# A decoder layer on one core: cross-attention's first steps with two pairs of projection banks, and the reload of the key norms in three steps

## Chip, cores and metric

The kernel runs on one core of one Trainium2 chip. The metric is device time in microseconds, the median of three runs; lower is better.

## What is computed

One pre-norm decoder layer on x (32 sequences of 64 tokens, 256 wide): self-attention with quantised projections, cross-attention over a context of 32 x 64 x 128, and a mixture of 8 experts, each added to x. The change touches cross-attention:

```python
q = (hidden_states @ Wq).reshape(B, Sq, H, D)          # H = 16 heads, D = 128
k = (encoder_hidden_states @ Wk).reshape(B, Skv, H, D)
v = (encoder_hidden_states @ Wv).reshape(B, Skv, H, D)
q = rmsnorm(q, gq)
k = rmsnorm(k, gk)
scores = jnp.einsum('bqhd,bkhd->bhqk', q, k) * scale
attn = jax.nn.softmax(scores, axis=-1)
out = jnp.einsum('bhqk,bkhd->bqhd', attn, v)
return out.reshape(B, Sq, H * D) @ Wo
```

The experts' part is `y = down(silu(gate(x)) * up(x))`, with weights of 8 experts that the kernel splits into two float16 halves (a high part and what is left of it) before it uses them.

## The kernel before

Three stages run one after another with a barrier between them: self-attention (0 to 229 us of the trace), cross-attention (230 to 625 us), experts (625 to 963 us).

Cross-attention handles 64 heads, numbered h: 4 groups of 512 tokens by 16 heads. Heads go in pairs. A loop over steps N from -9 to 32 is written out by hand for each engine; in step N the projections of pair m = N + 9 are made, the scores of pair n = N + 1, and the outputs of pair N. So the first eight steps, N = -9 to -2, only project pairs 0 to 7, which are the 16 heads of the first group; the step of N = -1 brings the first scores, and from N = 1 on every step has all parts.

For one head TensorE (PE) makes, in `query`, six matmuls of 512 columns into `bank_q`, and in `key` three into `bank_k` (L1051, L1059). ScalarE (ACT) squares the query bank and copies its high half (L857, L858), and squares the key bank (L864). VectorE (DVE) makes the query's low half (`query_low`, L960) and both halves of the key (`key_halves`, L964 and L966). In `squares` PE sums the squares into `bank_n` (L1071, 8 small matmuls in float32). There is one `bank_q` and one `bank_k`, so the query product of head h waits until DVE has read that of head h - 1 (`lq_done`), and the key product likewise (`lk_done`). The squares of the queries go to two buffers in turn, those of the keys to one, `sqk`. Accumulators `acc[0]` and `acc[1]` are two more banks, first written in the step of N = 1, by `project_out`.

**Pieces.** Beside this the experts' weights are prepared: 67 pieces of 128 x 512 float32, two for each step from N = -8 to N = 24 and one in N = 25. SyncE's queue (SP) loads a piece (`piece_load`, L765), ACT makes its high half (`piece_high`, L903), the low half comes from DVE for even pieces (L1003) and from GpSimd (POOL) for odd ones (two instructions, L826 and L828), and SP saves both halves to DRAM (`piece_save`, L769) and then at once loads piece i + 2 into the same buffer. There are two raw buffers, one for even and one for odd pieces. ACT does both pieces of a step at the step's start, ahead of everything else of that step.

**Key norms.** After 8 heads (a batch b, in the steps of m = 4, 8, ..., 32) ACT turns the summed squares into norms (L872, L876, and L883 for the queries). The keys' norms go through DRAM so that they come back spread over partitions: `key_norms(b)` on SP issues four saves (L777), waits until they have landed, and issues eight loads (L788, 128 KB each) into the tile `rec_k`, which lies in `ao`; two for each pair u. GpSimd multiplies them with the queries' norms (`both_norms`, L810), two steps ahead of the pair's scores in the first loop and three in the last steps.

SP's order in a step is: save even piece, load, save odd piece, load, and then `key_norms` where a batch is due. Whatever stands there holds up the saves and loads of the step behind it.

Of the kernel before, what the change touches and what calls it, by code (L numbers as in the profile page):

```python
# [24 lines left out]
LN_EPS = 1e-5  # L25


IDENT, ONES, SAMEB, POS, PICK0, PICK1, BEFORE, CONSTS = 0, 128, 256, 384, 448, 576, 704, 832

# [640 lines left out]
def cross_attention(nc, sem, over, dram, x_sb, cst, ao, hT, wq, wk, wvo, cT, ck):  # L670
# [6 lines left out]
    with ctx:  # L677
# [5 lines left out]
        kc = sb("x_kc", [P, P], F32)  # L683
        gains = sb("x_gains", [P, 5], F32)
        sqq = [sb(f"sqq{i}", [P, GN], F32) for i in range(2)]
        sqk = sb("sqk", [P, GN], F32)
        sc = [sb(f"x_sc{i}", [P, 2 * GT, S], F32) for i in range(2)]
        pf = sb("x_pf", [P, 2 * GT, S], F32)
        mx = [sb(f"x_mx{i}", [P, 2 * GT], F32) for i in range(2)]
# [60 lines left out]
        def bank_of(n):  # L750
            return bank_s if n <= TAIL else bank_n

        nc.clear_and_free_semaphores(over)
        with nc.Block() as block:

            @block.sync
            def _(sp):
                sp.dma_start(gains[:, 0:1], dram["gq2"].rearrange("(p a) -> p a", a=1)).then_inc(g_in, 16)
                sp.dma_start(gains[:, 1:2], dram["gk2"].rearrange("(p a) -> p a", a=1)).then_inc(g_in, 16)
                def piece_load(i):  # L760
                    if i == early:

                        sp.wait_ge(q_done, H2)
                        sp.wait_ge(k_done, H2)
                    sp.dma_start(raw(i), dram["wx"][:, i * PIECE:(i + 1) * PIECE]).then_inc(raw_in[i % 2], 16)  # L765

                def piece_save(i):
                    sp.wait_ge(low_odd if i % 2 else low_even, i // 2 + 1)
                    sp.dma_start(dram["w_hl"][:, :, i * PIECE:(i + 1) * PIECE].rearrange("l p n -> p l n"), halves(i)).then_inc(pair_out[i % 2], 16)  # L769
                    if piece(i + 2):  # L770
                        piece_load(i + 2)

                def key_norms(b):
                    g, first = b * HB // H2, b * HB % H2
                    sp.wait_ge(kc_done, b + 1)
                    for t in range(GT):
                        sp.dma_start(dram["key_norms"][g % 2].rearrange("b h t s -> t h b s")[t, first:first + HB],  # L777
                                     kc[32 * t + first:32 * t + first + HB, :].rearrange("h (b s) -> h b s", b=2)).then_inc(kc_saved, 16)
                    sp.wait_ge(kc_saved, (b + 1) * GT * 16)
                    if g:  # L780
                        sp.wait_ge(s_read, (b * HB - H2 + HB) // 2)
                    if b == 1:

                        for r in range(2):
                            sp.wait_ge(pair_out[r], early // 2 * 16)
# [66 lines left out]
            def _(act):  # L852
                def query(h):
                    act.wait_ge(q_done, h + 1)
                    if h >= 2:
                        act.wait_ge(ss_done, h - 1)
                    nc.scalar.activation(sqq[h % 2][:, :], bank_q, ACT.Square, scale=1.0 / (H_UP * W_UP)).then_inc(sq_done, 1)  # L857
                    nc.scalar.copy(q_hl[:, 0, slot(h), :], bank_q).then_inc(hq_done, 1)  # L858
# [90 lines left out]
            def _(dve):  # L949
# [7 lines left out]

                def query_low(h):
                    dve.wait_ge(hq_done, h + 1)
                    nc.vector.tensor_tensor(q_hl[:, 1, slot(h), :], bank_q, q_hl[:, 0, slot(h), :], ALU.subtract).then_inc(lq_done, 1)  # L960

                def key_halves(h):
                    dve.wait_ge(sq_done, h * 2 + 2)
                    nc.vector.tensor_scalar(k_hl[:, 0, slot(h), :], bank_k, gains[:, 2:3], None, ALU.mult).then_inc(hk_done, 1)  # L964
                    dve.wait_ge(hk_done, h + 1)
                    nc.vector.scalar_tensor_tensor(out=k_hl[:, 1, slot(h), :], in0=bank_k, scalar=gains[:, 2:3], in1=k_hl[:, 0, slot(h), :], op0=ALU.mult, op1=ALU.subtract).then_inc(lk_done, 1)  # L966

                def out_low(h):
                    dve.wait_ge(oh_done, h + 1)
# [73 lines left out]
            @block.tensor  # L1043
            def _(pe):
                def query(h):
                    if h:
                        pe.wait_ge(lq_done, h)
                    f, g = h % H2 * D2, h // H2
                    terms = [(k, a, b) for k in range(NCH) for a, b in TERMS]
                    for j, (k, a, b) in enumerate(terms):  # L1050
                        last = nc.tensor.matmul(bank_q, wq[:, a, k, f:f + D2], hT[:, g, b * NCH + k, :], start=(j == 0), stop=(j == len(terms) - 1))  # L1051
                    last.then_inc(q_done, 1)

                def key(h):
                    if h:
                        pe.wait_ge(lk_done, h)
                    f, g = h % H2 * D2, h // H2
                    for j, (a, b) in enumerate(TERMS):
                        last = nc.tensor.matmul(bank_k[:, :], wk[:, a, f:f + D2], cT[:, g, b, :], start=(j == 0), stop=(j == 2))  # L1059
                    last.then_inc(k_done, 1)  # L1060

                def squares(h):
# [3 lines left out]

                        pe.wait_ge(rq_done, h // HB)
                    pick = cst[:, PICKH + 31 - e:PICKH + 63 - e]
                    for i, sq in enumerate((sqq[h % 2], sqk)):
# [82 lines left out]
                for N in steps:  # L1152
# [490 lines left out]
def constants():  # L1643

    import numpy as np
    p, m, s = np.arange(P)[:, None], np.arange(P)[None, :], np.arange(S)[None, :]
    parts = [p == m, p >= 0 * m, p // S == m // S, p % S == s, p == m % S, p == S + m % S, p < m]
# [80 lines left out]
```

## Time and profile before

| what | value |
|---|---|
| median of 3 runs | 962.99 us (962.37 to 966.84) |
| profiled execution, its own time | 964.96 us |
| its span, first to last instruction | 963.2 us |
| mean granted TensorE clock | 0.921 of full |
| busy: PE / DVE / ACT / POOL | 787.8 / 632.4 / 535.6 / 386.0 us |
| the first eight steps of cross-attention | 233.2 to 301.4 us |

The profile lists for each engine when it was busy and, for each pause ahead of an instruction, what ended it. A pause matters where the engine in question, or one that waits for it, is the late one.

### The profile page before, as it was taken

The numbers are of one execution on the slowest core, as the hardware profiler recorded it, in microseconds if no ns is written. First come the engines' busy times: TensorE is split into PE (matmuls) and PEld (weight loads), VectorE is DVE, ScalarE is ACT, GpSimd is POOL, SyncE is SP. The second block draws the span as 40 slices with busy tenths as digits, with TensorE's granted clock in tenths as the row PEclk, the third lists the DMA queues.
The fourth block names the chain that finished last, engine by engine and source line by source line (L and its number), as shares of the span: only waits on it lengthen the run. The fifth ranks groups of instructions, "written<-read, shape, count | busy, mean of one in ns | idle before, by whom it ended". The sixth has DMA issues, their size and how long they took to land. (4 is left out here: it accounts for less than half of the span.)

```text
span 963.2 us, 29306 instructions
## 1 busy us (share of the span) xinstructions
PE 787.8 (82%) x11741; PEld 578.0 (60%) x11741; DVE 632.4 (66%) x1110; ACT 535.6 (56%) x1002; POOL 386.0 (40%) x445
## 2 busy tenths in 40 slices
PE   0599988864767999999999988862599999999992
PEld 0488878751323566566656656662477777777771
DVE  6788999553656899989999988667433333333330
ACT  1687878742545777676767664431155445445541
POOL 0231222320334555555555556300336555555542
PEclk9998999955998999999999989955799999999997
DMA  9110000000453444434243432092492222222223
GB/s 330 44 47 24 25 24 25 26 1 22 132 165 100 134 132 133 125 98 134 94 146 116 134 104 76 2 361 89 148 359 46 39 40 46 44 37 43 45 35 103
DMA packets 59402, 92.18 MB, mean 96 GB/s; under 512 B 6769, under 2 KB 39665, under 8 KB 59089
## 3 DMA queue, kind: packets, MB, share of 16 engines
q1 hardware_dynamic: 48048, 76.49, 23.9%
q0 software_dynamic: 7488, 10.23, 6.6%
q10 hardware_dynamic: 3744, 3.67, 1.1%
q8 instruction: 98, 1.61, 0.7%
q14 instruction: 24, 0.19, 0.1%
HBM read 63.36 MB, written 29.10 MB: 96 GB/s over the span
## 5 line engine op out<-in xcount | busy, mean ns | idle before, releaser
L1528 DVE SCALAR_TENSOR_TENSOR hid<-psu,hid 128x688 f32<-128x688 f32 x39 | 34.1, 875 | 146.3 <-ACT hid L1390 146.3
L1051 PE MATMUL xbank_qk<-arena 128*128 128x512 f16 x384 | 97.7, 392 | 20.8 <-DVE q_hl L960 15.8
L1146 PE MATMUL xbank_a<-arena,x_o 128*128 128x256 f16 x768 | 95.7, 275 | 2.8 <-DVE x_sb L999 1.7
L1390 ACT ACTIVATE hid<-psg 128x688 f32<-128x688 f32 x39 | 29.0, 744 | 117.3 <-PE psu L1597 117.3
L1612 PE MATMUL fbank<-arena,hidT 128*128 (+1 forms) x663 | 82.8, 273 | 0.8 <-ACT f_y L1410 0.8
L1146 PEld LDWEIGHTS xbank_a<-arena,x_o 128*128 128x128 f16 x768 | 72.6, 98 | 18.0 <-DVE x_o L970 7.8
L857 ACT ACTIVATE sqq<-xbank_qk 128x512 f32<-128x512 f32 x64 | 38.2, 597 | 78.0 <-PE xbank_qk L1051 78.0
L1597 PE MATMUL psg<-wgu,f_xT 128*128 x468 | 75.0, 310 | 4.0 <-ACT f_xT L1397 2.2
L1597 PE MATMUL psu<-wgu,f_xT 128*128 x468 | 74.6, 309 | 0.0
L1612 PEld LDWEIGHTS fbank<-arena,hidT 128*128 128x128 f16 (+1 forms) x663 | 62.9, 97 | 15.4 <-issue 9.2
L1051 PEld LDWEIGHTS xbank_qk<-arena 128*128 128x128 f16 x384 | 33.0, 99 | 63.2 <-DVE q_hl L960 23.9
L1364 POOL DMA_INDIRECT token_out<-f_y,f_to x39 | 62.6, 1604 | 17.3 <-issue 16.8
L1059 PE MATMUL xbank_qk<-cT,wk 128*128 128x512 f16 x192 | 53.5, 388 | 12.9 <-DVE k_hl L966 12.9
L817 POOL TENSOR_TENSOR x_pf<-x_sc,x_rden 128x512 f32<-128x512 f32 x32 | 33.4, 1043 | 75.5 <-DVE x_rden L993 75.5
L960 DVE TENSOR_TENSOR q_hl<-xbank_qk,q_hl 128x512 f16<-128x512 f32 x64 | 43.7, 682 | 24.0 <-ACT q_hl L858 24.0
L1597 PEld LDWEIGHTS psu<-wgu,f_xT 128*128 128x128 f16 x468 | 45.8, 98 | 22.5
L1597 PEld LDWEIGHTS psg<-wgu,f_xT 128*128 128x128 f16 x468 | 42.6, 98 | 27.7 <-issue 4.8
L826 POOL TENSOR_SCALAR arena<-arena 128x512 f32<-128x512 f32 x25 | 37.7, 1507 | 53.4 <-ACT x_pair L903 53.4
L964 DVE TENSOR_SCALAR k_hl<-xbank_qk,x_gains 128x512 f16<-128x512 f32 x64 | 47.8, 747 | 11.1 <-ACT sqk L864 11.1
L538 PE MATMUL bank_pt<-cst,sp 64*64 64x64 f32 x1024 | 42.2, 240 | 13.1 <-ACT pT L299 11.7
L1347 POOL COPY f_at<-f_from_all 128x1 uint32 (+1 forms) x39 | 27.1, 695 | 63.3 <-DVE f_from_all L1508 52.6
L966 DVE SCALAR_TENSOR_TENSOR k_hl<-xbank_qk,x_gains,k_hl 128x512 f16<-128x512 f32 x64 | 48.1, 751 | 2.3
(257 smaller groups left out, 1955.1 us busy)
## 6 DMA issues: line engine op xcount, KB each, us to landing
arena<-in_wx SPq DMA_DIRECT2D x51, 256.0 KB, 3.7
wgu<-w_hl SPq DMA_DIRECT2D x8, 1376.0 KB, 9.0
ao<-key_norms SPq DMA_DIRECT2D x64, 128.0 KB, 3.2
w_hl<-cT SPq DMA_DIRECT2D x26, 256.0 KB, 2.1
w_hl<-x_pair SPq DMA_DIRECT2D x25, 256.0 KB, 3.4
ao<-in_wx SPq DMA_DIRECT2D x16, 256.0 KB, 3.0
w_hl<-ao SPq DMA_DIRECT2D x16, 256.0 KB, 2.1
arena<-w_hl SPq DMA_DIRECT2D x8, 384.0 KB, 8.8
```

What stands on the lines that cost most here:

```text
L538: last = nc.tensor.matmul(pt[rows, n * S:(n + 1) * S], sp[i % 2][rows, 8 * part + n, :], cst[rows, IDENT + S * b:IDENT + S * b + S], start ...
L826: nc.gpsimd.tensor_scalar(raw(i), raw(i), W_UP, None, ALU.mult).then_inc(up_done, 1)
L857: nc.scalar.activation(sqq[h % 2][:, :], bank_q, ACT.Square, scale=1.0 / (H_UP * W_UP)).then_inc(sq_done, 1)
L960: nc.vector.tensor_tensor(q_hl[:, 1, slot(h), :], bank_q, q_hl[:, 0, slot(h), :], ALU.subtract).then_inc(lq_done, 1)
L964: nc.vector.tensor_scalar(k_hl[:, 0, slot(h), :], bank_k, gains[:, 2:3], None, ALU.mult).then_inc(hk_done, 1)
L966: nc.vector.scalar_tensor_tensor(out=k_hl[:, 1, slot(h), :], in0=bank_k, scalar=gains[:, 2:3], in1=k_hl[:, 0, slot(h), :], op0=ALU.mult, o ...
L1051: last = nc.tensor.matmul(bank_q, wq[:, a, k, f:f + D2], hT[:, g, b * NCH + k, :], start=(j == 0), stop=(j == len(terms) - 1))
L1059: last = nc.tensor.matmul(bank_k[:, :], wk[:, a, f:f + D2], cT[:, g, b, :], start=(j == 0), stop=(j == 2))
L1146: last = nc.tensor.matmul(acc[t // 2][:, (t % 2) * C:(t % 2 + 1) * C], o_hl[h % 2][:, a, at:at + P], wvo[:, b, e, :], start=(e == 0 and j ...
L1364: nc.gpsimd.indirect_dma_start(out=dram["token_out"], out_offset=bass.IndirectOffsetOnAxis(ap=to[:, 0:1], axis=0), in_=y[r ^ 1][:, :], in_ ...
L1597: last = nc.tensor.matmul(bank[:, c * 512:c * 512 + FH], xT[r][:, b * NCH + k, :], wgu[:, bass.ds(e, 1), at:at + FH].rearrange("p a n -> p ...
L1612: last = nc.tensor.matmul(ps[1][:, 0:C], hidT[r][0:rows, a, f, :], wd[0:rows, bass.ds(e, 1), at:at + C].rearrange("p a n -> p (a n)"), sta ...
```

## The change

- In the first eight steps the odd head of a pair is projected into `acc[0]` (query) and `acc[1]` (key) instead of `bank_q` and `bank_k`. A product of these steps waits for the reader of the head before the last (`banks_free`).
- PE's order in these steps: the key product of the odd head stands ahead of the squares of the even head.
- The keys' squares get a second buffer; ACT's key square waits for the sums of the head before the last, in all steps.
- `key_norms` is cut in three: saves in the batch's step, the loads of pairs u, u + 1 at the end of the next step, those of the other two pairs at the end of the one after.
- Four constant tables that nothing reads leave the constants' tile: 448 columns of 1113.

```diff
-IDENT, ONES, SAMEB, POS, PICK0, PICK1, BEFORE, CONSTS = 0, 128, 256, 384, 448, 576, 704, 832
+IDENT, ONES, BEFORE, CONSTS = 0, 128, 256, 384
...
-        sqk = sb("sqk", [P, GN], F32)
+        sqk = [sb(f"sqk{i}", [P, GN], F32) for i in range(2)]
...
+        def query_bank(h):
+            return acc[0][:, :] if h < H2 and h % 2 else bank_q
+
+        def key_bank(h):
+            return acc[1][:, :] if h < H2 and h % 2 else bank_k
+
+        def banks_free(h):
+            return h if h > H2 else h - 1
...
-                def key_norms(b):
+                def key_norms_out(b):
                     g, first = b * HB // H2, b * HB % H2
                     sp.wait_ge(kc_done, b + 1)
                     for t in range(GT):
...
+
+                def key_norms_in(b, part):
+                    g, first = b * HB // H2, b * HB % H2
                     sp.wait_ge(kc_saved, (b + 1) * GT * 16)
...
-                    for u in range(first // 2, (first + HB) // 2):
+                    for u in range(first // 2 + 2 * part, first // 2 + 2 * part + 2):
...
                     if batch(N) is not None:
-                        key_norms(batch(N))
+                        key_norms_out(batch(N))
+                    for part in range(2):
+                        if batch(N - 1 - part) is not None:
+                            key_norms_in(batch(N - 1 - part), part)
...
                 def key(h):
                     act.wait_ge(k_done, h + 1)
-                    if h:
-                        act.wait_ge(ss_done, h)
-                    nc.scalar.activation(sqk[:, :], bank_k, ACT.Square, scale=1.0 / (CTX_UP * W_UP)).then_inc(sq_done, 1)
+                    if h >= 2:
+                        act.wait_ge(ss_done, h - 1)
+                    nc.scalar.activation(sqk[h % 2][:, :], key_bank(h), ACT.Square, scale=1.0 / (CTX_UP * W_UP)).then_inc(sq_done, 1)
...
                 def query(h):
-                    if h:
-                        pe.wait_ge(lq_done, h)
+                    if banks_free(h) > 0:
+                        pe.wait_ge(lq_done, banks_free(h))
...
                 def key(h):
-                    if h:
-                        pe.wait_ge(lk_done, h)
+                    if banks_free(h) > 0:
+                        pe.wait_ge(lk_done, banks_free(h))
...
                         query(2 * m + 1)
+                        if m < NU:
+                            key(2 * m + 1)
                         squares(2 * m)
-                        key(2 * m + 1)
+                        if m >= NU:
+                            key(2 * m + 1)
```

The same order, as the engines get it. TensorE, one of the first eight steps, before (`xbank_qk` holds `bank_q` and `bank_k`, `xbank_n` is `bank_n`, `arena` holds the queries' weights and inputs):

```order
L1051 MATMUL xbank_qk<-arena 128x512 x6
L1059 MATMUL xbank_qk<-cT,wk 128x512 x3
L1051 MATMUL xbank_qk<-arena 128x512 x6
L1071 MATMUL xbank_n<-sqq,cst 32x128 x4
L1071 MATMUL xbank_n<-sqk,cst 32x128 x4
L1059 MATMUL xbank_qk<-cT,wk 128x512 x3
L1071 MATMUL xbank_n<-sqq,cst 32x128 x4
L1071 MATMUL xbank_n<-sqk,cst 32x128 x4
```

and in the changed kernel (`xbank_a` is the pair of accumulators; its line numbers are 16 higher here):

```order
L1067 MATMUL xbank_qk<-arena 128x512 x6
L1075 MATMUL xbank_qk<-cT,wk 128x512 x3
L1067 MATMUL xbank_a<-arena 128x512 x6
L1075 MATMUL xbank_a<-cT,wk 128x512 x3
L1087 MATMUL xbank_n<-sqq,cst 32x128 x4
L1087 MATMUL xbank_n<-sqk,cst 32x128 x4
L1087 MATMUL xbank_n<-sqq,cst 32x128 x4
L1087 MATMUL xbank_n<-sqk,cst 32x128 x4
```

The four products now stand together, and both sums of squares behind them.

SyncE's queue from the load that ends the step of m = 4 on, before (L765 loads a piece, L769 saves one, L777 and L788 save and load norms):

```order
L777 DMA key_norms<-x_kc 8x2x64 x4
L788 DMA ao<-key_norms 64x512 x8
L769 DMA w_hl<-ao 128x2x512
L765 DMA ao<-in_wx 128x512
L769 DMA w_hl<-ao 128x2x512
L765 DMA ao<-in_wx 128x512
L769 DMA w_hl<-ao 128x2x512
```

and in the changed kernel (L775 loads a piece, L779 saves one, L787 and L801 save and load norms):

```order
L787 DMA key_norms<-x_kc 8x2x64 x4
L779 DMA w_hl<-ao 128x2x512
L775 DMA ao<-in_wx 128x512
L779 DMA w_hl<-ao 128x2x512
L775 DMA ao<-in_wx 128x512
L801 DMA ao<-key_norms 64x512 x4
L779 DMA w_hl<-ao 128x2x512
L775 DMA ao<-in_wx 128x512
L779 DMA w_hl<-ao 128x2x512
L775 DMA ao<-in_wx 128x512
L801 DMA ao<-key_norms 64x512 x4
```

The eight loads that stood as one block ahead of the next piece's save now follow that step's and the next step's piece loads, four and four.

## Rows read from the trace of the kernel before

**Rows 1.** The page, its first part: TensorE, share of the span, instructions.
```profile
PE 787.8 (82%) x11741; PEld 578.0 (60%) x11741; DVE 632.4 (66%) x1110; ACT 535.6 (56%) x1002; POOL 386.0 (40%) x445
```

**Rows 2.** Busy time by stretch: PE, PEld, DVE, ACT, POOL (count), clock, DMA share, GB/s.
```profile
242.00:249.40 7.40, 5.47 (x54) 2.26 (x50) 4.99 (x8) 4.18 (x8) 2.64 (x2) 1.00 0.47 141
286.00:292.80 6.80, 6.11 (x42) 2.16 (x43) 2.99 (x5) 2.71 (x5) 1.01 (x1) 0.50 0.31 96
```

**Rows 3.** Waits in 233 to 301.4 us: total us, times, longest us.
```profile
PE xbank_qk L1051 <- DVE q_hl L960: 12.8, 8, 4.5
PE xbank_n L1071 <- ACT sqk L864: 5.5, 8, 0.7
```

**Rows 4.** Timeline, odd piece's loop; start us, us, engine, line [idle before <-releaser].
```profile
254.51 0.47 SPq L765 DMA_DIRECT2D ao<-in_wx  x1
...
257.57 0.63 ACT L903 ACTIVATE ao<-ao 128x512 f16<-128x512 f32 x1 [0.63 <-DMA ao<-in_wx]
...
258.28 1.65 POOL L826 TENSOR_SCALAR ao<-ao 128x512 f32<-128x512 f32 x1 [4.22 <-ACT ao L903]
...
260.01 1.15 POOL L828 TENSOR_TENSOR ao<-ao 128x512 f16<-128x512 f32 x1
...
261.61 0.47 SPq L765 DMA_DIRECT2D ao<-in_wx  x1
...
264.56 0.63 ACT L903 ACTIVATE ao<-ao 128x512 f16<-128x512 f32 x1 [0.20 <-DMA ao<-in_wx]
```

**Rows 5.** Timeline, first two pieces on ACT.
```profile
241.28 1.14 ACT L903 ACTIVATE ao<-ao 128x512 f16<-128x512 f32 x2
```

**Rows 6.** Timeline, the reload of the norms and what follows.
```profile
268.45 0.47 SPq L765 DMA_DIRECT2D ao<-in_wx  x1
268.96 1.41 SPq L777 DMA_DIRECT2D key_norms<-x_kc  x4
...
272.32 4.99 SPq L788 DMA_DIRECT2D ao<-key_norms  x8
...
279.02 0.56 SPq L765 DMA_DIRECT2D ao<-in_wx  x1
...
283.57 0.63 ACT L903 ACTIVATE ao<-ao 128x512 f16<-128x512 f32 x1 [0.65 <-DMA ao<-in_wx]
...
285.94 2.74 PE L1051 MATMUL xbank_qk<-arena 128*128 128x512 f16 x6 [4.52 <-DVE q_hl L960]
```

**Rows 7.** Line L765: landing of the load issued at 245.68, then of all 67.
```profile
DMA to landing us min/median/max: 4.9/4.9/4.9
...
DMA to landing us min/median/max: 2.8/3.6/5.3
```

**Rows 8.** Timeline, the step of N = -1 and the start of the next.
```profile
300.66 1.14 ACT L903 ACTIVATE ao<-ao 128x512 f16<-128x512 f32 x2
...
303.78 0.60 ACT L857 ACTIVATE sqq<-xbank_qk 128x512 f32<-128x512 f32 x1 [1.27 <-PE xbank_qk L1051]
...
310.98 0.95 PE L1099 MATMUL xbank_s<-k_hl,q_hl 128*64 128x64 f16 x48
```

**Rows 9.** Timeline, two pauses of TensorE and what follows each.
```profile
306.42 1.47 PE L1051 MATMUL xbank_qk<-arena 128*128 128x512 f16 x6 [1.92 <-DVE q_hl L960]
...
572.88 1.04 PE L1113 MATMUL xbank_s<-x_identh,x_p 128*128 128x128 f16 x8 [3.60 <-POOL x_p L822]
```

**Rows 10.** The page's GB/s in 40 slices; timeline, last stats of x.
```profile
GB/s 330 44 47 24 25 24 25 26 1 22 132 165 100 134 132 133 125 98 134 94 146 116 134 104 76 2 361 89 148 359 46 39 40 46 44 37 43 45 35 103
...
16.36 1.40 DVE L382 BATCH_NORM_STATS2 stats<-x_sb 128x6 f32<-128x256 f32 x4 [0.47 <-DMA x_sb<-in_x]
```

**Rows 11.** Timeline, a later piece that ACT waited for.
```profile
409.36 0.63 ACT L903 ACTIVATE cT<-arena 128x512 f16<-128x512 f32 x1 [1.09 <-DMA arena<-in_wx]
```

**Rows 12.** Timeline, the last save, and the product of norms 29.
```profile
590.77 0.37 SPq L769 DMA_DIRECT2D w_hl<-cT  x1
...
595.34 1.51 POOL L810 TENSOR_TENSOR ao<-ao,rec_q 128x512 f32<-128x512 f32 x1
```

More of the change, by code:

```diff
@@ L856, in query @@
                         act.wait_ge(ss_done, h - 1)
-                    nc.scalar.activation(sqq[h % 2][:, :], bank_q, ACT.Square, scale=1.0 / (H_UP * W_UP)).then_inc(sq_done, 1)
-                    nc.scalar.copy(q_hl[:, 0, slot(h), :], bank_q).then_inc(hq_done, 1)
+                    nc.scalar.activation(sqq[h % 2][:, :], query_bank(h), ACT.Square, scale=1.0 / (H_UP * W_UP)).then_inc(sq_done, 1)
+                    nc.scalar.copy(q_hl[:, 0, slot(h), :], query_bank(h)).then_inc(hq_done, 1)
                 def key(h):
                     act.wait_ge(k_done, h + 1)
-                    if h:
-                        act.wait_ge(ss_done, h)
-                    nc.scalar.activation(sqk[:, :], bank_k, ACT.Square, scale=1.0 / (CTX_UP * W_UP)).then_inc(sq_done, 1)
+                    if h >= 2:
+                        act.wait_ge(ss_done, h - 1)
+                    nc.scalar.activation(sqk[h % 2][:, :], key_bank(h), ACT.Square, scale=1.0 / (CTX_UP * W_UP)).then_inc(sq_done, 1)
                 def out_high(h):
@@ L959, in query_low @@
                     dve.wait_ge(hq_done, h + 1)
-                    nc.vector.tensor_tensor(q_hl[:, 1, slot(h), :], bank_q, q_hl[:, 0, slot(h), :], ALU.subtract).then_inc(lq_done, 1)
+                    nc.vector.tensor_tensor(q_hl[:, 1, slot(h), :], query_bank(h), q_hl[:, 0, slot(h), :], ALU.subtract).then_inc(lq_done, 1)
                 def key_halves(h):
                     dve.wait_ge(sq_done, h * 2 + 2)
-                    nc.vector.tensor_scalar(k_hl[:, 0, slot(h), :], bank_k, gains[:, 2:3], None, ALU.mult).then_inc(hk_done, 1)
+                    nc.vector.tensor_scalar(k_hl[:, 0, slot(h), :], key_bank(h), gains[:, 2:3], None, ALU.mult).then_inc(hk_done, 1)
                     dve.wait_ge(hk_done, h + 1)
-                    nc.vector.scalar_tensor_tensor(out=k_hl[:, 1, slot(h), :], in0=bank_k, scalar=gains[:, 2:3], in1=k_hl[:, 0, slot(h), :], op0=ALU.mult, op1=ALU.subtract).then_inc(lk_done, 1)
+                    nc.vector.scalar_tensor_tensor(out=k_hl[:, 1, slot(h), :], in0=key_bank(h), scalar=gains[:, 2:3], in1=k_hl[:, 0, slot(h), :], op0=ALU.mult, op1=ALU.subtract).then_inc(lk_done, 1)
                 def out_low(h):
@@ L1050, in query @@
                     for j, (k, a, b) in enumerate(terms):
-                        last = nc.tensor.matmul(bank_q, wq[:, a, k, f:f + D2], hT[:, g, b * NCH + k, :], start=(j == 0), stop=(j == len(terms) - 1))
+                        last = nc.tensor.matmul(query_bank(h), wq[:, a, k, f:f + D2], hT[:, g, b * NCH + k, :], start=(j == 0), stop=(j == len(terms) - 1))
                     last.then_inc(q_done, 1)
                 def key(h):
-                    if h:
-                        pe.wait_ge(lk_done, h)
+                    if banks_free(h) > 0:
+                        pe.wait_ge(lk_done, banks_free(h))
                     f, g = h % H2 * D2, h // H2
                     for j, (a, b) in enumerate(TERMS):
-                        last = nc.tensor.matmul(bank_k[:, :], wk[:, a, f:f + D2], cT[:, g, b, :], start=(j == 0), stop=(j == 2))
+                        last = nc.tensor.matmul(key_bank(h), wk[:, a, f:f + D2], cT[:, g, b, :], start=(j == 0), stop=(j == 2))
                     last.then_inc(k_done, 1)
@@ L1068, in squares @@
                     pick = cst[:, PICKH + 31 - e:PICKH + 63 - e]
-                    for i, sq in enumerate((sqq[h % 2], sqk)):
+                    for i, sq in enumerate((sqq[h % 2], sqk[h % 2])):
                         for t in range(GT):
@@ L1645, in constants @@
     import numpy as np
-    p, m, s = np.arange(P)[:, None], np.arange(P)[None, :], np.arange(S)[None, :]
-    parts = [p == m, p >= 0 * m, p // S == m // S, p % S == s, p == m % S, p == S + m % S, p < m]
+    p, m = np.arange(P)[:, None], np.arange(P)[None, :]
+    parts = [p == m, p >= 0 * m, p < m]
     c = np.concatenate([np.asarray(x, np.float32) for x in parts], axis=1)
```

## The prediction

> **What bounds the kernel now.** First the page: TensorE is busy 82% of the span [rows 1], so the question is where it is not. Two stretches of cross-attention's first steps answer it [rows 2]. From 242.0 to 249.4 us, one step of the eight (it runs from an even head's query product to the next even head's), TensorE works 5.47 of 7.4 us, VectorE 4.99, ScalarE 4.18, GpSimd 2.64: nobody is full, so a chain of waits sets the step. From 286.0 to 292.8 us the granted clock is 0.50, which is 1.2 GHz, half of the 2.4 GHz of the other. The view of waits names the chain [rows 3]: in these eight steps TensorE stood still 8 times, 12.8 us in all, ahead of a query product until VectorE had read the bank, and 8 times, 5.5 us, ahead of the squares until ScalarE had squared the key. The first kind is what a second pair of banks takes away.
>
> Then I look for a second loop nearly as long, because one that was hidden becomes the bound. It is the odd piece's [rows 4]: load issued at 254.51, ScalarE starts on it at 257.57, having stood 0.63 us for that transfer, GpSimd at 258.28 and again at 260.01, next load issued at 261.61 (1.6 us after the second GpSimd instruction's start, the save between them), ScalarE at 264.56, again after a wait, of 0.20 us. That is 7.0 us from one odd piece to the next, in a chain in which TensorE has no part; the step takes 7.4. ScalarE does its pieces at a step's start, ahead of all projections of the step, so it can't go faster than this loop.
>
> The third thing is the reload of the norms [rows 6]. SP issues the four saves at 268.96, then waits for them, and the eight loads start at 272.32 and take 4.99 us to issue. The odd piece's load comes at 279.02, 10.6 us after the one before it, of 268.45, its piece reaches ScalarE at 283.57, and TensorE, after a pause of 4.52 us, starts at 285.94 and needs 2.74 us for six matmuls that take 1.47 us at full clock [rows 9]. This one reload costs the late pieces and then the half clock.
>
> **The change, part by part.** Everything below is in the profiled execution, whose 964.96 us stand 1.97 above the median; the sum is a difference, and I take it off the median, 962.99.
>
> *Start of the chain.* ScalarE's first two pieces start at 241.28, the odd one some 0.5 us later, 241.8 [rows 5]. They stand behind the key square of head 1. In this step TensorE's second query product loses its wait (1.6 us in the mean [rows 3], of which I take 0.9 here, since the key product ahead of it still runs at the low clock), and the key product no longer stands behind the squares. Those take 0.5 us a head: 5.47 us less 18 long matmuls at 1.47 us for six leaves 1.06 for two heads [rows 2, 9]. So the first odd piece starts 1.4 us sooner, at **240.4**.
>
> *Seven turns of the odd loop.* Before, they took from 241.8 to 301.2 [rows 5, 8] (300.66, and 0.5 for the even one), 59.4 us. After, each is 7.0 us at least [rows 4]. One of the landings was slow, 4.9 us instead of the 3.0 usual here, and nothing of the change touches it [rows 7]: +1.8. For the load that runs beside the four saves of norms I add 0.4; for the two that start just ahead of or behind the blocks of four norm loads, 1.1 and 0.7 (their landing beside the eight was 4.5 us, 283.57 less 279.02 [rows 6], so 1.5 each is the upper end, nothing the lower). Together 49.0 + 1.8 + 2.2 = **53.0 us**, and 293.4 for the last odd piece instead of 301.2. Is SP free in time? Four loads of norms take half of 4.99, so 2.5 us; a step of 7 us has only four short issues beside, and by the loop's own times there are some 3 us between an odd load and the next even save. So the block of four just fits, and the reload's 3.6 us of lateness and the half clock behind it go. The wait for the saves to land is over a step later.
>
> *The step of N = -1.* Before, ScalarE's pieces here were not late; the query's square began at 303.78 and the next scores at 310.98, 7.2 us later [rows 8]. After, this step hangs on the odd piece: it is followed by 1.4 us of ScalarE (the piece, the logarithm, the exponential) and the same 7.2 us. So the next scores start at 240.4 + 53.0 + 8.6 = **302.0 instead of 310.98: 9.0 us less.**
>
> *A pause that is new.* Head 17 is past the double banks and waits for the reader of head 16, which now waits for the late odd piece. TensorE is there a step ahead, so I work out a pause of 3.8 to 4.0 us. After 3.60 us it came back at half clock (eight transposes in 1.04 us [rows 9]), after 1.92 us at full clock. Six matmuls at half clock cost 1.27 more, part of it beside VectorE's work: **+0.6**, with 0 and 2 as ends.
>
> *Steady steps, N = 0 to 23.* TensorE bounds them and their products keep one pair of banks. What goes is a late piece behind some reloads: ScalarE waited 1.09 us at 409.36 [rows 11], and a like amount once more. I take **-0.7**, between 0 and -2.3. The second `sqk` buffer I cost at nothing: the wait it relaxes, for sums that TensorE makes before the key product it follows, was always over.
>
> *Tail.* The last batch's second block of loads now stands behind the last save, at 590.77 [rows 12]. Pair 30 needs it; pair 29 was at 595.34 and a step is over 5 us, so it is due at about 600.7. Two issues and a landing, by 595.6: **0**, with 5 us to spare.
>
> *Constants.* 448 columns of 4 bytes on 128 partitions are 229 KB; at the 330 GB/s of the first slice 0.7 us, and VectorE waited 0.47 us for the last of x [rows 10]: **-0.5**, between 0 and -0.7.
>
> Sum: -9.0 + 0.6 - 0.7 - 0.5 = **-9.6 us, so 953.4** (about 955.4 if the profiled execution again stands 2 above).
>
> The Trainium skill (DMA: Bandwidth & Descriptors, the formula by its section on the anatomy of one DMA) gives 2.0 us and the bytes at 436 GB/s for a transfer from another queue, 2.6 us as an estimate for a piece of 256 KB. The landings here are longer, 3.0 us, with a median of 3.6 over all [rows 7], and by the page's figure seven turns would be 2.8 us shorter and the sum 950.6; the traced ones are used.
>
> **The rivals.**
>
> *The loads get slower, not only sooner.* Pieces, saves and norm loads come closer together on the same DMA queues. If each odd load lands in 4.5 us, as beside the reload, a turn takes 8.5 us and seven take 59.5, as long as before. What is left is 1.4 at the start, 1.2 in the step of N = -1, and the 1.2 of the small parts: 3.8, so 959.2. For it: the median landing over all is 3.6, the worst 5.3 [rows 7]. Against: DMA share was only 0.47 in such a step [rows 2]. Within this lies that the banks bring nothing.
>
> *The loop is never late.* No landing over 3.0 us: turns of 7.0, 49.0 us, the next scores at 298.0, 13.0 less, and 1.2 from the small parts: 948.8.
>
> *The clock falls for all of the first steps.* TensorE would wait in one long pause per step instead of two short ones. If those pauses reach the 3.6 us after which it was found at 1.2 GHz, the products of a step cost 2 x 1.27 and 2 x 0.65 us more and the squares some 0.9, nearly twice their 1.06: a step of 5.5 + 4.7 = 10.2 us of TensorE, eight of them 82 us instead of the 68.2 from 233.2 to 301.4. That is 13.4 more, 12.2 with the 1.2 of the small parts taken off: 975.2. It decides from pauses of 3.6 us in each step on; I work out 1.6 to 2.8 at the longest, and a pause of 1.92 left the clock up [rows 9]. At half clock there would also be no pauses left. The Trainium skill (TensorE: Matmul & The Clock Gate, A second HAM failure mode: psum-queue depth-cycling) reports a kernel whose cycling through PSUM banks each iteration made TensorE pause often enough for its clock to swing between the two levels. By that page this change would come out slower; the trace has steps with two pauses each at full clock (1.00 in rows 2), which speaks against it here.
>
> **How the numbers follow.** The forecast 0.68, slower loads 0.12, never late 0.17, the clock 0.03. The range of 8 in 10 takes in the forecast with its bounds and most of the case of no late loads: 948.5 to 957.5. What a measurement of this kernel can tell from no change is about 0.5%, 4.8 us. The forecast and the case of no late loads are beyond it but for a small tail; slower loads are within: faster 0.86, same 0.11, slower 0.03.
>
> **What would show it.** In the changed profile: ScalarE's waits for pieces in the first steps grow in number, to about one per step, and TensorE's waits for VectorE there fall below 5 us (besides the one of head 17); odd pieces stand 7.0 to 8 us apart; the clock is 1.00 from 245 to 290; next scores (the second L1099 group) near 302; no gap of 10 us between odd loads. I am wrong if odd pieces stand under 6.9 apart (then the loop isn't what I read), if the clock is 0.5 anywhere between, or if time comes from beyond 311 us.

## The result

The changed kernel takes 954.15 us (median of 4 runs, 952.4 to 955.66), the kernel before 964.18 us (4 runs, 962.37 to 966.84). The ratio is 0.989, 95% interval 0.987 to 0.991. The forecast was 953.4, the range 948.5 to 957.5. Beside the experiments the change was run once more: 954.53 us, ratio 0.990 (0.988 to 0.992). Its trace is called the second trace of the change below.

The page of the changed kernel, its head, its first part's first row and the granted clock in 40 slices:

```profile
span 953.1 us, 29312 instructions
PE 789.0 (83%) x11741; PEld 582.9 (61%) x11741; DVE 629.9 (66%) x1110; ACT 533.9 (56%) x1002; POOL 385.0 (40%) x445
...
PEclk9999788975999999999999989955799999999996
```

The span is 10.1 us shorter than 963.2, and TensorE is busy for 789.0 us, 1.2 more than in [rows 1]. So what went is waiting, not work. Where they went is read from the starts of five instructions that stand at the same place in both programs:

| stretch | before, us | after, us | difference |
|---|---|---|---|
| start to cross-attention's first matmul | 233.19 | 235.04 | +1.85 |
| from there to the scores of pair 1 | 77.79 | 67.41 | -10.38 |
| to the scores of pair 24 (steady steps) | 252.86 | 252.19 | -0.67 |
| to the experts' first transfer (SP) | 61.91 | 61.58 | -0.33 |
| to the end | 337.45 | 336.88 | -0.57 |

The second row is the change. In the second trace of the change it is 68.53 us, 9.26 less than before. Its steps, by the view of busy time by stretch (columns as in [rows 2]): one of the best, one as the odd loop makes them, and the one of m = 4 (each from an even head's query product to the next even head's):

```profile
242.40:248.06 5.66, 5.22 (x54) 2.43 (x51) 4.63 (x8) 3.95 (x8) 2.64 (x2) 1.00 0.49 148
254.37:261.17 6.80, 5.28 (x54) 2.43 (x51) 4.70 (x8) 4.07 (x8) 2.64 (x2) 1.00 0.51 155
261.17:272.17 11.00, 7.05 (x55) 2.91 (x51) 5.47 (x9) 5.25 (x12) 2.64 (x2) 0.84 0.48 146
```

TensorE works 5.2 to 5.3 us in the first two, a little less than the 5.47 of [rows 2]; the step is 5.66 us where nothing is late, 6.80 where the odd piece is, and 11.00 where its landing was slow, part of it at half clock. The waits from cross-attention's first matmul to the scores of pair 0 (235 to 291 us), beside [rows 3]:

```profile
ACT ao L919 <- DMA ao<-in_wx: 14.1, 8, 4.0
PE xbank_n L1087 <- ACT sqk L880: 7.0, 11, 1.4
```

The 12.8 us in which TensorE waited for VectorE ahead of a query product are gone without rest. In their place ScalarE waits 8 times for a piece, 14.1 us instead of the 6.4 of before (5 times; L903 for `ao`, 233 to 301.4 us), and TensorE 11 times for ScalarE's key square, 7.0 us. The chain has moved from the banks to the transfers. One turn of the odd loop, beside [rows 4] (ScalarE's two pieces of a step, GpSimd's two instructions, SP's load, ScalarE's next odd piece):

```profile
253.59 0.67 ACT L919 ACTIVATE ao<-ao 128x512 f16<-128x512 f32 x1
256.99 0.63 ACT L919 ACTIVATE ao<-ao 128x512 f16<-128x512 f32 x1 [2.73 <-DMA ao<-in_wx]
...
257.71 1.49 POOL L842 TENSOR_SCALAR ao<-ao 128x512 f32<-128x512 f32 x1 [4.07 <-ACT ao L919]
259.28 1.15 POOL L844 TENSOR_TENSOR ao<-ao 128x512 f16<-128x512 f32 x1
...
260.88 0.47 SPq L775 DMA_DIRECT2D ao<-in_wx  x1
...
265.10 0.63 ACT L919 ACTIVATE ao<-ao 128x512 f16<-128x512 f32 x1 [4.04 <-DMA ao<-in_wx]
```

The odd piece starts at 256.99, GpSimd's second instruction at 259.28, and the next load at 260.88: 3.89 us from piece to load, where [rows 4] have 4.04 (GpSimd's first instruction took 1.65 us there, 1.49 here). ScalarE waits 2.73 us for the piece where it had waited 0.63. The next one comes at 265.10 only, after a wait of 4.04: its load took 4.2 us to land. That load, the one of piece 7, is late in each trace that has the second pair of banks and GpSimd in the odd loop: 4.2 to 4.7 us in five traces, against 2.9 to 3.0 in the three traces of the kernels with one pair and the same loop (before, constants alone, reload alone). So it comes with the change; what slows it, no run here shows. Odd pieces start at 242.2, 250.19, 256.99, 265.10, 271.9, 279.26, 286.77 and 293.88: seven turns, 51.7 us, against 59.4. In the second trace of the change they take 53.4 us.

SP's queue at the first reload, beside [rows 6]: saves of the norms, first block of four loads, a piece's save, second block, a piece's save.

```profile
269.50 1.40 SPq L787 DMA_DIRECT2D key_norms<-x_kc  x4
...
276.35 2.45 SPq L801 DMA_DIRECT2D ao<-key_norms  x4
279.59 0.38 SPq L779 DMA_DIRECT2D w_hl<-ao  x1
...
284.27 2.37 SPq L801 DMA_DIRECT2D ao<-key_norms  x4
286.68 0.59 SPq L779 DMA_DIRECT2D w_hl<-ao  x1
```

The first block ends at 278.80, before the next save at 279.59 is due. The second ends at 286.64 and the save follows at 286.68; its piece's low half had been ready at 285.65, so that save was held up by 1.0 us. The longest distance between two odd loads is now 8.1 us instead of 10.6 (260.88 to 268.99), and the half clock behind the reload is gone.

The end of the first steps, beside [rows 8]: the last odd piece, the query product of head 17, the scores of pair 1.

```profile
293.88 0.63 ACT L919 ACTIVATE ao<-ao 128x512 f16<-128x512 f32 x1 [2.49 <-DMA ao<-in_wx]
...
296.95 2.74 PE L1067 MATMUL xbank_qk<-arena 128*128 128x512 f16 x6 [1.05 <-DVE q_hl L976]
...
302.45 0.95 PE L1115 MATMUL xbank_s<-k_hl,q_hl 128*64 128x64 f16 x48
```

8.57 us from the piece to the scores.

### The profile page after: what moved, and what is told of

Read it like the earlier page. It is cut to its first block and busy times, and to the rows that moved or that the text cites. A ratio compares the mean times of both kernels' runs of the same rounds, so it can differ in the third digit from the quotient of the medians.

```text
span 953.1 us, 29312 instructions
## 1 busy us (share of the span) xinstructions
PE 789.0 (83%) x11741; PEld 582.9 (61%) x11741; DVE 629.9 (66%) x1110; ACT 533.9 (56%) x1002; POOL 385.0 (40%) x445
## 5 line engine op out<-in xcount | busy, mean ns | idle before, releaser
L1067 PE MATMUL xbank_qk<-arena 128*128 128x512 f16 x336 | 84.8, 390 | 6.3 <-DVE x_gains L971 3.9
L873 ACT ACTIVATE sqq<-xbank_qk 128x512 f32<-128x512 f32 x56 | 33.3, 595 | 60.5 <-PE xbank_qk L1067 60.5
L1075 PE MATMUL xbank_qk<-cT,wk 128*128 128x512 f16 x168 | 46.8, 389 | 12.7 <-DVE k_hl L982 12.7
L1067 PEld LDWEIGHTS xbank_qk<-arena 128*128 128x128 f16 x336 | 28.8, 99 | 39.6 <-DVE q_hl L976 4.8
L976 DVE TENSOR_TENSOR q_hl<-xbank_qk,q_hl 128x512 f16<-128x512 f32 x56 | 38.1, 681 | 20.5 <-ACT q_hl L874 20.5
L218 POOL TENSOR_SCALAR kd<-cst,deq 128x128 f32<-128x128 f32 x16 | 11.8, 738 | 89.0 <-PE bank_g L584 61.0
L980 DVE TENSOR_SCALAR k_hl<-xbank_qk,x_gains 128x512 f16<-128x512 f32 x56 | 41.8, 747 | 8.8 <-ACT sqk L880 8.8
```

The costliest lines, as they stand in the source:

```text
L976: nc.vector.tensor_tensor(q_hl[:, 1, slot(h), :], query_bank(h), q_hl[:, 0, slot(h), :], ALU.subtract).then_inc(lq_done, 1)
L980: nc.vector.tensor_scalar(k_hl[:, 0, slot(h), :], key_bank(h), gains[:, 2:3], None, ALU.mult).then_inc(hk_done, 1)
L1067: last = nc.tensor.matmul(query_bank(h), wq[:, a, k, f:f + D2], hT[:, g, b * NCH + k, :], start=(j == 0), stop=(j == len(terms) - 1))
L1075: last = nc.tensor.matmul(key_bank(h), wk[:, a, f:f + D2], cT[:, g, b, :], start=(j == 0), stop=(j == 2))
```

## The experiments

Each ratio is against the kernel before, run beside it on the same chip. Three chips were used, and the kernel before took 963.60, 964.67 and 965.13 us on them, so kernels of different chips are better compared by ratio or by stage than by their medians. The chips are given as a, b and c. The stage here is the stretch of the table's second row, from cross-attention's first matmul to the scores of pair 1, read from each run's one trace: 77.8 us before, 67.4 and 68.5 us in the two traces of the change.

| run | chip | median, us | ratio (95%) | stage, us |
|---|---|---|---|---|
| constants alone | a | 963.49 | 1.000 (0.998 to 1.002) | 77.8 |
| reload in three steps alone | a | 958.21 | 0.994 (0.991 to 0.996) | 70.7 |
| banks (and constants) | a | 958.34 | 0.994 (0.992 to 0.996) | 71.4 |
| change, GpSimd's low half twice | a | 961.63 | 0.998 (0.996 to 1.000) | 76.5 |
| change once more | b | 954.53 | 0.990 (0.988 to 0.992) | 68.5 |
| change, odd low halves on VectorE | b | 947.87 | 0.983 (0.981 to 0.986) | 60.6 |
| change, double banks to head 17 | b | 953.22 | 0.990 (0.987 to 0.992) | 67.3 |
| both of these | b | 948.60 | 0.984 (0.982 to 0.987) | 59.7 |
| reload in three, odd low halves on VectorE | c | 957.03 | 0.992 (0.989 to 0.994) | 71.0 |

### The constants alone

```diff
-IDENT, ONES, SAMEB, POS, PICK0, PICK1, BEFORE, CONSTS = 0, 128, 256, 384, 448, 576, 704, 832
+IDENT, ONES, BEFORE, CONSTS = 0, 128, 256, 384
```

> The kernel before with the four unused constant tables dropped and nothing else. The traces of before and of the change show the first statistics on VectorE 0.5 to 0.8 us sooner, and a self-attention that then takes 2.7 us longer in the one profiled execution. If the shorter transfer is all, this gains 0.5 to 0.8 us. If the moved addresses of the tiles make self-attention slower (the rival), it is 1 to 2 us slower than before.

Measured: 1.000 of before, 0.998 to 1.002. That is up to 1.9 us of gain or 1.8 of loss; it excludes only the rival's upper end of 2 us, and settles nothing else. The traces say a little more. In the changed kernel's, VectorE makes the last statistics without the pause of [rows 10], and the step behind them starts sooner (view: timeline):

```profile
12.66 4.25 DVE L382 BATCH_NORM_STATS2 stats<-x_sb 128x6 f32<-128x256 f32 x12
16.95 1.17 DVE L389 BATCH_NORM_AGGREGATE mv<-stats 128x2 f32<-128x6 f32 x16
```

The aggregation starts at 16.95; before it was at 17.80. In the single traces it is at 16.8 to 17.8 us with the short constants (eight, mean 17.1) and at 17.4 to 17.8 with the long ones (three, mean 17.5): 0.4 us, less than its own scatter. Cross-attention then begins at 231.1 to 235.0 us in the eight traces with short constants (mean 232.6) and at 233.2 to 234.4 in the three with the long ones (mean 233.8). The scatter of self-attention is larger than the gain. Every kernel here with the second `sqk` buffer, which takes 2048 bytes of a partition, also has the short constants, which give up 1792; so the banks were not tried without them.

### Each half of the change alone

Reload in three steps, everything else as before:

```diff
-                def key_norms(b):
+                def key_norms_out(b):
...
+                def key_norms_in(b, part):
...
-                    for u in range(first // 2, (first + HB) // 2):
+                    for u in range(first // 2 + 2 * part, first // 2 + 2 * part + 2):
...
-                        key_norms(batch(N))
+                        key_norms_out(batch(N))
+                    for part in range(2):
+                        if batch(N - 1 - part) is not None:
+                            key_norms_in(batch(N - 1 - part), part)
```

> The kernel before with only the reload of the norms cut in three; one pair of banks, old constants. My theory: the late pieces after the first reload and the half clock behind them go, so pair 6 to pair 7 takes a step of 7.4 instead of 13.5 us, and 0.7 us come from the steady steps: 7 to 8 us faster than before, which is most of the whole change. Rival, that the banks carry the gain: 2 us or less.

The reverse, the changed kernel with that diff undone:

> The changed kernel with the reload in one block again (two pairs of banks, two sqk buffers, short constants). The odd piece's loop and the block of eight loads still set the pace: some 1.4 us at the start, 1 to 2 in the step of N = -1 and up to 2 from the loop's 7.0 against 7.4, and TensorE still waits over 4 us after the reload and comes back at half clock: 3 to 6 us faster than before, 0.6 of it from the constants. Rival, that two banks make steps of 5.65 us as in the changed trace's best ones: 8 us or more.

The first gains 0.6% (0.4 to 0.9), some 6 us, the second 0.6% (0.4 to 0.8), 5.5 us. The second expectation held; the first had 7 to 8 us, which the interval reaches. The stages, each read from one trace, point the same way: 7.1 us less by the reload, 6.4 by the banks, 9.3 to 10.4 by both. They overlap, by 3 to 4 us. The waits in the first steps, of the reload's kernel:

```profile
PE xbank_qk L1057 <- DVE q_hl L966: 9.7, 8, 1.3
ACT ao L909 <- DMA ao<-in_wx: 3.1, 6, 1.1
```

TensorE still waits for VectorE 8 times, 9.7 us: the steps are 7.4 us each, none longer. And of the banks' kernel:

```profile
ACT ao L913 <- DMA ao<-in_wx: 17.7, 7, 4.6
PE xbank_n L1081 <- ACT sqk L874: 8.5, 10, 2.9
```

No bank wait, but 17.7 us of waiting for pieces. Its reload, on SP, ScalarE and TensorE (the eight loads, the odd piece's load, that piece on ScalarE, TensorE's next squares):

```profile
270.93 4.99 SPq L798 DMA_DIRECT2D ao<-key_norms  x8
277.61 0.56 SPq L775 DMA_DIRECT2D ao<-in_wx  x1
...
281.98 0.63 ACT L913 ACTIVATE ao<-ao 128x512 f16<-128x512 f32 x1 [0.75 <-DMA ao<-in_wx]
...
284.12 0.66 PE L1081 MATMUL xbank_n<-sqq,cst 128*32 128x128 f32 x8 [2.86 <-ACT sqk L874]
```

The load at 277.61 stands behind the eight, its piece starts at 281.98 and TensorE has paused 2.86 us, where it paused 4.52 in [rows 6]; the expectation had over 4. It came back at half clock, as expected: these eight small matmuls take 0.66 us instead of 0.43 at full clock. TensorE had made all four products of the step before the late piece started, since they fit in two pairs of banks. That is the overlap: the banks soften the very stall that the new reload takes away.

The reload's edit does two things at once: it moves the norm loads behind the piece loads of the next steps, and it cuts the block of eight in two. No run has one without the other, so which of them is needed is open.

### The odd loop made longer, and shorter

Longer: GpSimd writes the same low half twice for the pieces of the first steps (a wait between the two).

```diff
+                    if i < early:
+                        nc.gpsimd.tensor_tensor(halves(i)[:, 1, :], raw(i), halves(i)[:, 0, :], ALU.subtract).then_inc(again, 1)
+                        pool.wait_ge(again, i // 2 + 1)
                     nc.gpsimd.tensor_tensor(halves(i)[:, 1, :], raw(i), halves(i)[:, 0, :], ALU.subtract).then_inc(low_odd, 1)
```

> The changed kernel with GpSimd writing the low half of each odd piece of the first eight steps twice (1.15 us more in each turn of the odd loop, nothing else on any other engine). If the loop sets the pace of these steps, each of seven turns is about 1.2 us longer: 7 to 9 us slower than the change. If the projections do, GpSimd with 4 us of work in a step of 7 hides it: within 1 us of the change.

Measured: 961.63 us, ratio 0.998, where the change has 0.990: some 7.6 us slower. The stage is 76.5, 8 to 9 us longer. The timeline on ScalarE and GpSimd shows one turn (odd piece, low half, low half again, next odd piece):

```profile
255.97 0.63 ACT L923 ACTIVATE ao<-ao 128x512 f16<-128x512 f32 x1 [4.16 <-DMA ao<-in_wx]
...
258.26 1.15 POOL L846 TENSOR_TENSOR ao<-ao 128x512 f16<-128x512 f32 x1
259.49 1.16 POOL L848 TENSOR_TENSOR ao<-ao 128x512 f16<-128x512 f32 x1
...
265.28 0.63 ACT L923 ACTIVATE ao<-ao 128x512 f16<-128x512 f32 x1 [5.25 <-DMA ao<-in_wx]
```

The added 1.23 us on an engine that works 3.8 us in a step of over 8 goes into the turn undiminished: seven turns of the odd pieces take 60.8 us, 9.1 more than in the first trace of the change and 7.4 more than in the second, which is 1.1 to 1.3 a turn. So the loop sets the pace.

Shorter: VectorE makes the low halves of the odd pieces 1 to 13, in one instruction.

```diff
+ON_DVE = 14
...
                 def piece_low(i):
+                    if i < ON_DVE:
+                        return
                     pool.wait_ge(high_done, i + 1)
...
-                    pool.wait_ge(up_done, i // 2 + 1)
+                    pool.wait_ge(up_done, (i - ON_DVE) // 2 + 1)
...
                     if piece(piece_at(N, 0)):
                         piece_low(piece_at(N, 0))
+                    if 0 <= piece_at(N, 1) < ON_DVE:
+                        piece_low(piece_at(N, 1))
```

(VectorE's `piece_low` increments `low_odd` for odd pieces.)

> The changed kernel with the low halves of odd pieces 1 to 13 made by VectorE in one instruction, as the even ones are, instead of by GpSimd in two. The odd loop is then a load of 3.0, 0.6 to VectorE, 0.7 and 0.7 to the save and 0.4 to the next load, about 5.5 us, and ScalarE's and TensorE's own chain of 5.65 us a step sets the pace, or VectorE with 5.7. If the loop is what bounds the first steps, six to seven turns get 1 to 1.5 us shorter: 6 to 9 us faster than the change. If the transfers themselves are the bound (rival), or VectorE becomes it, 2 us or less.

The mark beside it:

> The changed kernel once more, as the mark for the three beside it: 0.988 to 0.991 of the time before.

Measured: 947.87 us, 6.7 below the change in the same rounds and 1.7% below before (1.4 to 1.9). This version beats both kernels. Its busy time by stretch, two of the first steps:

```profile
240.20:245.80 5.60, 5.16 (x53) 2.38 (x51) 5.16 (x9) 4.04 (x8) 0.00 (x0) 1.00 0.54 169
252.20:257.80 5.60, 5.16 (x53) 2.38 (x51) 5.53 (x10) 3.67 (x7) 0.00 (x0) 1.00 0.45 137
```

Here the pace of the pieces on ScalarE (L922):

```profile
253.29 0.63 ACT L922 ACTIVATE ao<-ao 128x512 f16<-128x512 f32 x1 [1.25 <-DMA ao<-in_wx]
...
259.87 0.63 ACT L922 ACTIVATE ao<-ao 128x512 f16<-128x512 f32 x1 [0.75 <-DMA ao<-in_wx]
```

These steps take 5.6 us, TensorE works 5.16 of them and VectorE 5.53 of the second, so there is little left to take out of such a step. But these two pieces stand 6.6 us apart; over seven turns it is 45.5 us, 6.5 each instead of the 7.6 of the change beside it (53.4). The expectation had a turn of 5.5 with a landing of 3.0 us; the odd loads of these turns landed in 3.4 to 5.1 us, 4.0 in the mean, which accounts for the 1.0 us a turn by which it was off.

The same edit where the banks wait, on the kernel with the reload in three steps:

> The kernel of e2 (one pair of banks, reload in three steps) with the same edit as e6, the low halves of odd pieces 1 to 13 on VectorE. If the odd loop became the bound only through the second pair of banks, it is hidden here behind the bank waits of a 7.4 us step: within 1.5 us of e2 either way, about 0.993 of before, and the first eight steps still take some 61 us. If the loop bounded the steps before as well (rival), this gains 4 us or more on e2.

Measured: 957.03 us against 958.21 for that kernel without the edit, on another chip; the ratios are 0.992 (0.989 to 0.994) and 0.994 (0.991 to 0.996). They differ by some 2 us, well inside the two intervals, so no gain is shown, and a small one isn't excluded. The stage, 71.0 and 70.7, has none, and the rival's 4 us did not come. Its waits:

```profile
PE xbank_qk L1062 <- DVE q_hl L969: 10.0, 8, 1.6
ACT ao L912 <- DMA ao<-in_wx: 2.9, 3, 1.4
```

Pieces cost ScalarE 2.9 us here and the bank waits are still 10.0 (9.7 without the edit). In the stage the same edit is worth nothing before the second pair of banks and 8 us after it (68.5 to 60.6).

These two kernels also show what the shorter loop does to the transfers. Without the edit four of the odd loads were issued 2.6 us behind the even one and landed in 2.9 to 3.1 us; with it the seven were issued 1.0 to 1.5 us behind it and landed in 3.6 to 5.7 us. So work taken out of the loop crowds its transfers together, and part of the gain goes back into their landings.

### One more step of double banks

```diff
+DOUBLE = H2 + 2
...
-            return acc[0][:, :] if h < H2 and h % 2 else bank_q
+            return acc[0][:, :] if h < DOUBLE and h % 2 else bank_q
...
-            return h if h > H2 else h - 1
+            return h if h > DOUBLE else h - 1
...
-                        if m < NU:
+                        if m < DOUBLE // 2:
```

(and the same for `key_bank` and the second condition).

> The changed kernel with one more step of double banks: heads 16 and 17 too, the accumulators being free until the next step. The pause that head 17 makes TensorE wait behind the late odd piece and VectorE's reading of head 16 goes: the step of N = -1, from the odd piece to the next scores, takes about 6.5 us instead of 8.6, 2 us faster than the change. Rival: ScalarE has as much to do there anyway, or the gain is eaten by the next step's late piece: under 0.7 us.

Measured: 953.22 us, 1.3 below the change beside it, with intervals that are nearly the same; not told apart. From the odd piece to the scores it took 7.07 us, where the two traces of the change have 8.57 and 7.75. The timeline of ScalarE and TensorE shows what is late in the bank's place (odd piece; copy of the quotient; the key square of head 17; the scores of pair 1):

```profile
291.33 0.63 ACT L920 ACTIVATE ao<-ao 128x512 f16<-128x512 f32 x1 [2.27 <-DMA ao<-in_wx]
...
296.66 0.62 ACT L913 CAST x_p<-x_pf 128x512 f16<-128x512 f32 x1 [0.87 <-POOL x_pf L834]
297.18 0.59 ACT L881 ACTIVATE sqk<-xbank_a 128x512 f32<-128x512 f32 x1
...
298.40 0.95 PE L1116 MATMUL xbank_s<-k_hl,q_hl 128*64 128x64 f16 x48
```

The key product stood ready in its bank from 295.30 on, but ScalarE's order has the copy L913 ahead of it, and that waited for GpSimd. The medians' 1.3 us lie between the rival's 0.7 and the 2 us that I expected, and decide nothing; by the trace the step is 0.7 to 1.5 us shorter, not 2.

> The changed kernel with both: low halves of odd pieces 1 to 13 on VectorE, double banks up to head 17. If both terms are as read, the two gains add up: 8 to 11 us faster than the change, near 944 to 946. If the next steps' own loop (odd pieces from 15 on are GpSimd's again) takes it back, 6 us or less.

Measured: 948.60 us against 947.87 without the double banks of head 17: 5.9 us below the change, so the 8 to 11 us that I expected did not come and the rival of 6 us or less did. That the later odd pieces take the gain back, as the rival says, is not shown. The stage is 59.7 us instead of 60.6, 0.9 less; the medians don't show it.

## Why the prediction was right

*Bank waits go, and the odd loop is next.* Right. 12.8 us of waits went, and [rows 4]'s loop showed in its place, 3.89 us from piece to load instead of 4.04. The two experiments that stretch and shorten it, and the third, in which shortening it leaves the stage as it was, show this rather than argue it.

*Start of the chain.* The first odd piece was forecast 7.2 us behind the first matmul (240.4 less 233.2) and came 7.1 behind (242.2 less 235.0), 7.3 in the second trace.

*Seven turns, 53.0 us.* 51.7 and 53.4 measured. The parts were not those I set. A turn without any late landing takes 6.80 us and not 7.0, with a load that lands in 2.9. The load with the slow landing of [rows 7] was slow again, 4.1 us instead of 4.9 (4.2 in the second trace), but a second one was slow too, 4.2 us (4.5), the one of piece 7 above, for which I had nothing. The odd loads that stand ahead of the two blocks of norm loads landed in 3.4 and 3.6 us, 0.5 and 0.7 above 2.9, where I had 1.1 and 0.7; in the second trace in 4.0 and 3.4.

*The step of N = -1, 8.6 us.* 8.57 in one trace, 7.75 in the other. *The new pause* I had sized at 3.8 to 4.0 us in one piece. It was 1.63 and 1.05 with a transpose and three matmuls between, because the transpose of the norms waits for ScalarE as well; TensorE did come back at half clock, 2.74 us for six matmuls. In the second trace the same product took 1.47 us behind one pause of 1.02, and that is part of the difference between 8.57 and 7.75. The forecast for the stretch was 8.6 and 0.6, 9.2 in all: the pause cost nothing on top of the 8.6.

*Longest pauses elsewhere, 1.6 to 2.8 us.* Wrong: in the step of m = 4 it was 3.50, with half clock behind it (transpose and key product, in the timeline):

```profile
266.15 0.47 PE L1094 MATMUL xbank_n<-cst,x_logs 128*128 128x128 f32 x1 [3.50 <-ACT x_logs L888]
266.41 1.49 PE L1075 MATMUL xbank_qk<-cT,wk 128*128 128x512 f16 x3
```

The second trace has 3.79 us there, and half clock too. That step took 11.00 us. What I had missed is the transpose of the norms: in the steps of m = 4 and m = 8 TensorE needs logarithms for it that ScalarE makes behind the late piece of the same step, so the lead that TensorE has elsewhere doesn't help it. The loop did not get longer by the half clock: the turn that holds it, 265.10 to 271.9, takes 6.8 us, as little as any.

*Steady steps, -0.7.* -0.67, and -0.54 in the second trace. *Tail, 0.* Right: -0.33 in all from pair 24 to the experts, +0.30 in the second trace. The second block of loads stands behind the last save, at 581.72, and the product of norms 30, the first that needs it, comes 7 us after its last issue and has no wait for it (SP and GpSimd):

```profile
581.72 2.36 SPq L801 DMA_DIRECT2D ao<-key_norms  x4
...
591.20 1.50 POOL L826 TENSOR_TENSOR ao<-ao,rec_q 128x512 f32<-128x512 f32 x1
```

*Constants, -0.5.* In its own place 0.84 us in the profiled execution and 0.4 in the mean over the traces; further on it is lost in the scatter: in the profiled execution cross-attention began 1.85 us later than before, in the second trace 0.42 us later. The busy time by stretch of the kernel before at 100 to 120 us:

```profile
100.00:120.00 20.00, 17.61 (x438) 16.38 (x434) 18.60 (x36) 16.62 (x35) 5.50 (x5) 0.91 0.09 29
```

and of the changed one:

```profile
100.00:120.00 20.00, 17.59 (x312) 15.96 (x310) 16.01 (x30) 14.09 (x32) 5.52 (x4) 0.64 0.09 29
```

The granted clock is 0.64 instead of 0.91 in this stretch, in instructions that the change doesn't touch. The second trace of the change has 0.91 there, and so have seven of the eight traces of the other experiments; one has 1.00. It is scatter between executions. The 27 executions of the kernel before on chip a fit this: the two slowest, 969.28 and 968.44 us, had a mean clock of 0.914 and 0.916, the two with the highest clock, 0.926, took 962.35 and 963.59. Which of the two makes the other is not shown.

*The clock for all of the first steps, 975.2.* It did fall twice there in the changed kernel, each time behind a late piece, and was 1.00 in the two other steps shown above, which cycle through the same four banks. What the Trainium skill tells of a kernel that cycles through banks (TensorE: Matmul & The Clock Gate, A second HAM failure mode: psum-queue depth-cycling) did not decide here. *The loop's period.* By the Trainium skill's figure for a transfer from another queue (DMA: Bandwidth & Descriptors, Anatomy of one DMA) it would have been 6.6 us and the sum 950.6, as estimated; the turns were 6.8 at the least and 7.4 in the mean, nearer to the traced 7.0.

*The signs of being wrong.* Two of the three came, both small. Two turns were 6.80 us, under the 6.9 that I had named: the loop is the one I read, 0.2 us shorter. And from 266 us on a key product and part of the query product behind it ran at half clock, after the pause of 3.50 us. Here the loop held and the price of TensorE's pauses was what I had wrong. Of the third, time from beyond 311 us, there were 1.6 us of the 10.1, 0.9 more than forecast.

*The rivals.* Slower loads (959.2) and never late (948.8) did not come; the measured time lies between them, 0.8 us from the forecast. Part of this nearness is luck. From the first matmul to the scores of pair 1 the sum had 8.4 us less; the two traces have 10.4 and 9.3 less. The constants were to give 0.5 us, and the medians show nothing of it; cross-attention even began later in both traces. The one made up for the other.

## What to carry to other kernels

Before a bank wait is taken out of a step, write down each loop that passes through the same in-order engine, transfers included, with its period: here 7.0 us stood behind a step of 7.4, and the second pair of banks could not gain more than that difference a step, apart from stalls and the two ends. A shortening of that hidden loop did nothing to these steps while the first wait was there (71.0 us against 70.7), and afterwards took 6.7 us off the kernel, no less than the banks had (some 5.5). Such a loop also doesn't shrink by all that is taken out of it, when its transfers then land later. And a block of loads that an in-order queue issues in 5 us holds up the transfers queued behind it and all that waits for them: moved behind them and cut in two, the same loads left the stage 7.1 us shorter. Look also for the steps in which the engine that runs ahead is tied to the late one, as by the norms' transpose here: there its lead is gone.

## What was not expected of the hardware

TensorE came back at half clock without one long pause. In the step of N = -1 above, head 17's product took 2.74 us after pauses of 1.63 and 1.05 us with about 1 us of work between them, while after one pause of 1.92 us it came back at full clock [rows 9]. But short pauses in a row don't always do it: with the reload in one block the same product took 1.47 us after pauses of 1.33 and 1.06. And in the second trace of the change it was head 16's product that took 2.74 us, after pauses of 1.25 and 0.82, where the first trace has 1.47 after 1.37 and 0.82. So with nearly the same pauses the clock falls in one execution and not in another, and these traces don't say what decides.

The clock in self-attention, too, differs between executions of one kernel: 0.64 and 0.91 between 100 and 120 us in the two traces of the change. TensorE was busy 17.59 us in both, but got through 312 instructions in the one and 444 in the other.
